# Attention block on one core: compressed and selected probabilities in 24 to 80 columns a head, transposed two or four heads at a time, against values laid out at the matching rows

## What is computed

```python
ck, cv = weighted sums of 16-token blocks of k, v (plus a position term)   # 64 blocks
a_comp = masked_softmax(q @ ck.T, block finished before the token)         # up to 64 columns
a_sel  = masked_softmax(q @ k_sel.T, token not before the key)             # 16 columns
a_win  = masked_softmax(q @ k.T, the last 128 tokens)
out = g0 * (a_comp @ cv) + g1 * (a_sel @ v_sel) + g2 * (a_win @ v)
```

## Time and profile before

| what | value |
|---|---|
| three runs shown | 2268.36, 2272.89, 2275.06 us, median 2272.89 |
| span of the profiled execution | 2265.8 us; no time is given for this execution by itself |
| PE, PEld | 2108.9 us (93%), 1398.6 us (62%) |
| DVE, ACT, POOL | 1698.7 us (75%), 1331.8 us (59%), 792.1 us (35%) |
| cs transposes (L645) | 1024 matmuls, in 256 groups of four |
| cs copies (L1127) | 256, of which 224 from the spare bank: 133.0 us |
| the three stretches | prologue to about 156 us, seven batches of 268.7 us, epilogue from about 2036 us |

### The profile page before, as it was taken

The page is one execution under the profiler, slowest core; times in us unless marked ns, Lnnn a source line. Parts: engine busy times, 40 slices in busy tenths (PEclk is TensorE's granted clock), DMA queues, the critical chain, the costliest instruction groups (busy, mean ns, idle before and its releaser), DMA issues.

```text
span 2265.8 us, 49116 instructions
## 1 busy us (share of the span) xinstructions
PE 2108.9 (93%) x17948; PEld 1398.6 (62%) x17948; DVE 1698.7 (75%) x4741; ACT 1331.8 (59%) x4706; POOL 792.1 (35%) x780
## 2 busy tenths in 40 slices
PE   6989999999999999999999999999999999997887
PEld 3656666566665666656665666656666566664454
DVE  4667777777876887777887777777787688776775
ACT  2346666656664665656665665655666566565554
POOL 2433333433334333333343333343333333333121
PEclk9999999999999999999999999999999999998999
DMA  6110000200011000110002000020001100021000
GB/s 219 55 34 25 20 29 29 70 30 29 24 49 55 25 20 30 52 47 29 29 24 75 29 19 26 29 70 29 29 25 52 52 25 20 29 52 38 20 21 19
DMA packets 49022, 89.66 MB, mean 40 GB/s; under 512 B 6888, under 2 KB 6888, under 8 KB 48784
## 3 DMA queue, kind: packets, MB, share of 16 engines
q1 hardware_dynamic: 37520, 68.95, 9.9%
q10 hardware_dynamic: 11264, 17.57, 2.1%
HBM read 69.68 MB, written 16.83 MB: 38 GB/s over the span
## 4 chain that ended last, share of the span: by engine, by line
PE 57%; DVE 26%; ACT 7%; issue 6%; POOL 3%; DMA 1%; SPq 0%; DVEq 0%; POOLq 0%; ACTq 0%
PE ps_m L719 9%; PE ps_o L651 7%; PE ps_m L684 5%; ACT pw L1093 5%; DVE ps_s L1632 4%; PE ps_s L645 4%; PE ps_m L523 4%; PE ps_m L525 4%; PE ps_m L524 4%; PE ps_t L627 4%; DVE wmax L1637 3%; PE ps_m L701 3%; PE ps_s L603 2%; DVE cden L1692 2%; DVE pT L1660 2%
## 5 line engine op out<-in xcount | busy, mean ns | idle before, releaser
L1093 ACT ACTIVATE pw<-ps_s,wmax 128x128 f32<-128x128 f32 x1024 | 359.1, 379 | 241.1 <-DVE wmax L1637 240.1
L523 PE MATMUL ps_m<-w_hi,h_hi 128*128 128x512 f32 x768 | 368.1, 479 | 4.0 <-DVE h_lo L1763 1.4
L1103 ACT ACTIVATE pw<-pw,wden 128x128 f32<-128x128 f32 x1024 | 313.8, 401 | 6.5 <-DVE wden L1647 6.1
L525 PE MATMUL ps_m<-w_hi,h_lo 128*128 128x512 f32 x768 | 303.6, 395 | 0.0
L524 PE MATMUL ps_m<-w_lo,h_hi 128*128 128x512 f32 x768 | 303.6, 395 | 0.0
L684 PE MATMUL ps_m<-wo_s,aT 128*128 128x512 f32 x512 | 259.3, 628 | 6.4 <-ACT v_s L1058 3.7
L719 PE MATMUL ps_m<-wbt_s,h2T 128*128 128x512 f32 x512 | 252.2, 612 | 0.0
L1127 ACT ACTIVATE pT<-ps_s 80x512 f32<-80x512 f32 (+6 forms) x224 | 133.0, 594 | 182.2 <-PE ps_s L645 171.5
L1093 ACT ACTIVATION_READ_ACCUMULATOR pw<-ps_s,wmax 128x1 f32 x1024 | 224.6, 219 | 0.0
L1658 DVE COPY_PREDICATED pT<-keep_prev,ps_t 128x512 f32<-128x512 uint32 x224 | 163.8, 731 | 52.9 <-PE ps_t L627 51.5
L1345 POOL TENSOR_TENSOR css<-css,cm 128x256 f32<-128x256 f32 (+7 forms) x128 | 110.9, 887 | 258.6 <-DVE cm L1684 258.6
(11 more groups left out here) (196 smaller groups left out, 4219.5 us busy)
## 6 DMA issues: line engine op xcount, KB each, us to landing
xa<-x_in SPq DMA_DIRECT2D x65, 256.0 KB, 2.9
xc<-x_in SPq DMA_DIRECT2D x64, 256.0 KB, 2.7
out<-t ACTq DMA_DIRECT2D x64, 256.0 KB, 2.1
wo_s<-wo_in SPq DMA_DIRECT2D x8, 1024.0 KB, 9.3
wbt_s<-wbt_in SPq DMA_DIRECT2D x8, 1024.0 KB
gbc<-gate_rows SPq DMA_DIRECT2D x24, 256.0 KB, 5.2
pw<-wmod_in SPq DMA_DIRECT2D x3, 1024.0 KB, 8.0
pT<-wmod_in SPq DMA_DIRECT2D x3, 1024.0 KB, 9.2
```

The costliest lines, as they stand in the source:

```text
L523: pe_.matmul(ps[:], h_hi[:, c, :], w_hi[:, col, c, :], start=(c == 0), stop=False)
L525: mm = pe_.matmul(ps[:], h_lo[:, c, :], w_hi[:, col, c, :], start=False, stop=(c == NC - 1))
L1093: ins = act.activation(pw[:, hw, :], ps_w[:, j, i, 1, :], ACT.Exp, bias=wmax[:, hw:hw + 1], accum_out=wden[:, 0, hw:hw + 1])
L1103: act.activation(pw[:, hw, :], pw[:, hw, :], ACT.Copy, scale=wden[:, 2, hw:hw + 1]).then_inc(wn_ok, 1)
```

## The change

- `css` holds the heads at a width that depends on the tile (`head_width`): 32 columns for tiles 0 and 1, 64 for tiles 2 to 5, 80 for tiles 6 and 7, the heads in the order of their group. `csp` is gone; exponentials and scaling happen in place, `cs_exps` and `cs_mask` are one instruction each.
- A transpose takes 128 columns, four heads at a width of 32 and two at 64, and one head's 72 or 80 columns in tiles 6 and 7. So a tile needs 1, 2 or 4 rounds of four transposes and a copy (`rounds_of`), 18 a batch where there were 32. `transpose_cs` and `probs_copy` return at once for rounds that a tile doesn't have; the calls stay where they were.
- A head's probabilities then lie at rows 32j or 64(j mod 2), so its values must lie there too: `cs_values` reads `cv_four` (tiles 0 and 1), `cv_two` (tiles 2 to 5) or `csv` (6 and 7). SP makes these copies of `csv` by six DMAs a batch, 512 KB (`spread_values`, L447 and L449 of the new kernel), put at the head of a batch's loop; `cs_values` of tile 0 waits for them (`d_cv`).
- `compress` writes the values at rows 16 to 79 in three strips of 32 instead of two, `select_values` adds to the first strip, and one ACT copy replaces two.

```diff
+def head_width(t):
+    return 32 if t < 2 else 64 if t < 6 else CS
+def rounds_of(t):
+    return 1 if t < 2 else 2 if t < 6 else 4
...
+            def spread_values(b):
+                sp.wait_ge(cv_done, b + 2)
+                for k in range(2):
+                    sp.dma_start(cv_two[64 * k:64 * k + 64, :], csv[0:64, :]).then_inc(d_cv, 16)
+                for k in range(4):
+                    sp.dma_start(cv_four[32 * k:32 * k + 32, :], csv[0:32, :]).then_inc(d_cv, 16)
             def batch(b, a):
                 for s in range(1, NT):
+                    if s == 1:
+                        spread_values(b)
...
-            def transpose_cs(b, t, g):
+            def transpose_cs(b, t, r):
+                if r >= rounds_of(t):
+                    return
...
-                rows = P - NB + blocks_seen(t)
-                for j in range(4):
-                    mm = pe_.transpose(dst[0:rows, j, :], csp[:, NC * j + g, 0:rows], ident)
+                wide, rows = (P, P) if w < CS else (CS, NSEL + blocks_seen(t))
+                for k in range(4):
+                    at = wide * (4 * r + k)
+                    mm = pe_.transpose(dst[0:rows, k, :], css[:, at:at + rows], ident)
...
-            def cs_values(b, t, g):
-                add_values(g, csv, pT_cs[:, g % 2], False, True, P - NB + blocks_seen(t)).then_inc(pvc_done, 1)
+            def cs_values(b, t, c):
+                if t == 0 and c == 0:
+                    pe_.wait_ge(d_cv, 16 * REPLICAS * (b + 1))
...
+                    src, at, part = ((cv_four, 32 * j, c) if rounds == 1 else
+                                     (cv_two, 64 * (j % 2), 2 * (c % 2) + j // 2) if rounds == 2 else (csv, 0, j))
+                    mm = pe_.matmul(ps_o[HD * j:HD * j + HD, c, :], src[at:at + n, cols], pT_cs[at:at + n, k % 2, part, :],
+                                    start=False, stop=True, skip_group_check=True)
...
-                act.activation(csp[:, :, 0:NSEL], css[:, :, 0:NSEL], ACT.Exp).then_inc(cs_exp, 1)
-                n = blocks_seen(t)
-                act.activation(csp[:, :, P - NB:P - NB + n], css[:, :, NSEL:NSEL + n], ACT.Exp).then_inc(cs_exp, 1)
+                v = heads(t)[:, :, 0:NSEL + blocks_seen(t)]
+                act.activation(v, v, ACT.Exp).then_inc(cs_exp, 1)
...
-                for p in range(2):
-                    ins = dve.tensor_tensor(css[:, 8 * p:8 * p + 8, 0:n].rearrange("p (j c) n -> p j c n", j=2),
-                                            ps_s[:, 2 * p:2 * p + 2, 0:4 * CS].rearrange("p j (c n) -> p j c n", c=4)[:, :, :, 0:n],
-                                            mask, ALU.add)
+                dve.tensor_tensor(css[:, 0:H * head_width(t)].rearrange("p (c j n) -> p c j n", c=NC, j=4)[:, :, :, 0:n],
+                                  ps_s[:, :, 0:4 * CS].rearrange("p j (c n) -> p j c n", c=NC)[:, :, :, 0:n],
+                                  csmask[:, t, 0:n].unsqueeze(1).unsqueeze(1).broadcast_to([P, 4, NC, n]), ALU.add
+                                  ).then_inc(s_done, 1)
```

More of the change, by code:

```diff
@@ L151, in blocks_seen, with rounds_before, values_through, value_strip @@
     return (t + 1) * (P // CB)
-def t_spare(t, g):
-    return t > 0
+def head_width(t):
+    return 32 if t < 2 else 64 if t < 6 else CS
+def rounds_of(t):
+    return 1 if t < 2 else 2 if t < 6 else 4
+def rounds_before(T):
+    per = [rounds_of(t) for t in range(NT)]
+    return T // NT * sum(per) + sum(per[:T % NT])
+def values_through(k):
+    b, r = divmod(k, rounds_before(NT))
+    t = max(u for u in range(NT) if rounds_before(u) <= r)
+    return 4 * (NT * b + t) + (r - rounds_before(t) + 1) * 4 // rounds_of(t)
+def value_strip(t):
+    return divmod(NSEL + t * (P // CB), 32)
 def program(nc, x, wqkv, wo, wbt, wa, wb, cT, wmod, bo, bg, rb, wcomp, pe, pet, wg, const, gscr, out):
@@ L224, in program @@
         csv = sb("csv", [P, D])
+        cv_two = sb("cv_two", [P, D])
+        cv_four = sb("cv_four", [P, D])
         csk = sb("csk", [P, NC, CS])
@@ L554, in compress @@
                     pe_.wait_ge(s_done, QUADS * ba + quad(0, 1) + 2)
-                    for k in range(2):
-                        pe_.matmul(strip[k], pew[:, 0:per], pe_s[:, :], start=True, stop=False, skip_group_check=True)
+                    for k in range(3):
+                        at = NSEL if k else 0
+                        pe_.matmul(ps_cv[32 * k:32 * k + 32, :], pew[:, at:at + 32], pe_s[:, :], start=True, stop=False,
+                                   skip_group_check=True)
                 for t in tiles:
-                    if t == half - 1:
+                    if t == NT - 1:
                         pe_.wait_ge(*m_done_at(seg, b, "V", NT - 1))
[L560 to L565, removed]
+                    k, row = value_strip(t)
+                    off = NB - 8 - row
+                    pe_.matmul(ps_cv[32 * k:32 * k + 32, :], blkw[:, off:off + 32], v_s[:, t, :], start=False,
+                               stop=(t in (5, 7)), skip_group_check=True)
             def importance(ba):
@@ L1119, in copy_zT, with probs_copy @@
                 act.activation(zT[:, :], ps[0:NZ + 1, 0:P], ACT.Copy).then_inc(done, 1)
-            def probs_copy(b, t, g):
-                n = 4 * (NT * b + t) + g
-                act.wait_ge(tc_full, n + 2)
-                if g >= 2 or t > 0:
-                    act.wait_ge(pvc_done, n)
-                rows = P - NB + blocks_seen(t)
-                act.activation(pT_cs[0:rows, g % 2], (spare_t if t_spare(t, g) else ps_t)[0:rows], ACT.Copy).then_inc(tc_done, 1)
+            def probs_copy(b, t, r):
+                if r >= rounds_of(t):
+                    return
+                k = rounds_before(NT * b + t) + r
+                act.wait_ge(tc_full, k + 2)
+                if k >= 2:
+                    act.wait_ge(pvc_done, values_through(k - 2) + 1)
+                rows = P if head_width(t) < CS else NSEL + blocks_seen(t)
+                act.activation(pT_cs[0:rows, k % 2], (spare_t if t else ps_t)[0:rows], ACT.Copy).then_inc(tc_done, 1)
             def copy_out(b, t):
@@ L1689, in cs_factor @@
                 base = CS_STEPS * T
-                dve.wait_ge(cs_exp, 2 * T + 3)
-                for w, (lo, n) in enumerate(((0, NSEL), (P - NB, blocks_seen(t)))):
-                    dve.tensor_reduce(cden[:, w, :], csp[:, :, lo:lo + n], AX.X, ALU.add).then_inc(cs_ok, 1)
+                dve.wait_ge(cs_exp, T + 2)
+                for w, (lo, hi) in enumerate(parts(t)):
+                    dve.tensor_reduce(cden[:, w, :], heads(t)[:, :, lo:hi], AX.X, ALU.add).then_inc(cs_ok, 1)
                 dve.wait_ge(cs_ok, base + 6)
```

96 lines of the change are left out of this document (48 added, 48 removed).

## The result

The changed kernel takes 2319.95 us (median of 4 runs, 2318.94 to 2324.0) against 2272.1 us of the kernel before (4 runs): 1.0214 times the time, 95% interval 1.0199 to 1.0228. That is 48 us slower, where 11.7 us faster was forecast.

The account below looks back on a forecast made before the run. The prediction took PE as the bound, with waits for DVE. Its terms, -6.2 - 2.0 + 3.2 - 2.7 - 4.0 = -11.7 us, took 2272.9 to 2261 us, range 2249 to 2279.

Parts of the forecast that it names:

- What bounds the kernel: PE first, busy 93% of the span; work taken from it counts only where PE is late, as it sometimes awaits DVE.
- signs that were to show me wrong: Slots 2 to 5 losing over 0.6 us or gaining time, PE waiting over 3 us, or cv_four values far over 0.22.
- First slot, tile 0: cs_values 0 waits for the six copies, delaying the next scores by 0.53 us in six batches: +3.2 us.
- the rival of late copies: The six copies reach first-slot cs_values 0 late; 4.2 us instead of 0.7 would give 2282 us; chance 0.24.
- Slots 2 to 5: 28 loop slots: 0.55 us won at the window's last transposes, 0.33 lost to changes of shape behind: -6.2 us.
- The prices: On PE, a group of four cs transposes takes 0.44 us and each change of matmul shape costs 0.11.
- ACT's copies at nothing: 14 fewer ACT copies a batch, 112 x 0.6 us, counted as no gain in the loop because ACT has time there.
- the turn at nothing: At the turn, three compression strips side by side instead of two, and six more SP issues, were to cost nothing.
- Tile 1: In the first slot, the second norm's transposes come 0.38 us sooner, later savings and shape changes cancelling: -2.7 us.
- The mask: One DVE instruction for two saves 0.07 us at the head of slots 2, 5, 6 and 7: -2.0 us.
- The epilogue: Last batch's slots: -1.4 us in the first slot, smaller gains in tile 1 and later slots: -4.0 us in all.
- Strips on different rows: Rival: cs_values strips on different rows don't run side by side, 70 us more, giving 2321 us; chance 0.08.

Follow-up runs that it names:

- run 1: Changed kernel with SP issuing the six copies of the compressed values ahead of the feed-forward weights instead of behind: 2287.73 us, ratio 1.0055.
- run 3: Changed kernel with the packing undone: all tiles in four rounds of 80 columns, values at one set of rows, no copies: 2293.89 us, ratio 1.0083.
- run 5: Kernel of run 3 with cs_values of tiles 2 to 5 reading 72 rows instead of 40 to 64: 2280.63 us, ratio 1.0016.
- run 2: Changed kernel with POOL's product of the keys held behind DVE's second norm in first slot and turn: 2309.88 us, ratio 1.0155.
- run 4: Kernel before with ACT's copy of the keys ahead of the second copy of compressed probabilities in the first slot: 2279.22 us, ratio 1.0017.
- run 9: Changed kernel with edits of run 1 and run 2, cs_values 0 and 1 before the window's last transposes, DVE's t before the gates' second half: 2262.78 us.

## Why the prediction was wrong, by its steps

- **What bounds the kernel**: right as a rule, not carried through. I had written that work taken from PE counts only where PE is late, and then looked at one bank. Two of the signs that were to show me wrong came: slots 2 to 5 got longer, and in the first slot PE waited over 3 us (3.99).
- **First slot, tile 0** (+3.2, measured +27.7) is the step with most of the error. The mechanism was named, as the rival of late copies, and weighed too lightly. I had sized the copies by bytes at 373 GB/s, and let only 0.26 MB of their 0.52 count; behind the weights they cost 2.5 us, 212 GB/s. I had also read the end of the old transfers from the bytes, 972.2, where `xa` landed at 972.95. The issues were mis-sized too, 4.5 us for six where I had 2.4, but they were over 3.9 us before the last copy landed and did not set it. `cs_values` started 1.9 us later than forecast, 3.3 later than before, and I had no term for the clock, which took 1 us more after the stop of 4 us (run 1: both go together).
- **Slots 2 to 5** (-6.2, measured +8.6). The prices were right: changes of shape at 0.11 us, three of them behind the wait, and with the 0.02 behind each they account for run 3 and run 5. The gain of 0.55 was the wrong step. It was real at the first bank (27.55 to 27.01), but 0.43 us behind it stands a second one that DVE gives back only at 27.9, so 0.08 was left. DVE's timeline had that row; I asked for the wait of the next instruction and not of the one behind.
- **ACT's copies at nothing, the turn at nothing** (measured +0.9 us in tile 1 and +0.85 in the turn, 12 us): here I asked what ACT's absence would cost and not what it would set off. ACT's earlier copy let POOL start into DVE's norm (runs 2 and 4). The Trainium skill says this plainly (SBUF — State Buffer, SBUF: two separate sides): the second pair of ports of DVE, which GpSimd shares, is an exclusive lock for a whole instruction, where the DVE instruction uses two ports or reads two operands from SBUF. The trace agrees: 1.48 us for 0.55, ending behind POOL's 1.27; that the norm is such an instruction, no run shows by itself. It was a rule against this change that I did not weigh. Its clause that the one that starts first gets the lock holds only roughly by the starts in the profile, which are rough for POOL: DVE lost it with a lead of 0.05 to 0.10 us. Why POOL came some hundredths earlier in the turn stays open.
- **Tile 1** (-2.7): at full clock and without the collision it took 23.97 us (run 2) for 24.04, so 0.07 of the 0.38 was there. The norm's transposes came 0.28 us earlier (11.52 us after the slot's start for 11.80), but the changes of shape behind them were not paid for by the third group, as I had it: 0.21 went again.
- **The mask**: the price was right, 1.49 us for the pair's 1.55 in tile 7. Slot 6 is 0.11 us shorter; slot 7 with the turn, without the collision (run 2), is not (62.87 for 62.82), so how much of the 2.0 us was paid stays open.
- **The epilogue** (-4.0, measured +1.1): its first slot also waits for the copies. In run 1 it takes 20.64 us for 21.87, close to the -1.4 forecast; the slots behind it vary by more than a microsecond with the clock in all kernels, so the rest can't be told.
- **Strips on different rows** run side by side: that rival fell. By the Trainium skill (TensorEngine Tiling, Gotcha 1: PSUM Pressure) different row tiles cannot use one bank at the same time; here two or four of them wrote one bank, at other partitions, 7 ns one after the other as in the kernel before, with no such price.

## What to carry to other kernels

Where work is taken from the bounding engine, follow it to the next two or three banks that another engine has to give back; the gain ends at the first that is late, and it came here only with the edit that made that engine earlier (run 9). A small copy is priced by what stands ahead of it in its queue, not by its bytes alone, and the stop of 4 us that it made on PE cost 1 us of clock on top. An engine that gets faster off the path starts something earlier: look at what runs on the other engines at that moment, above all POOL against DVE.

## What the runs showed of the hardware

- A DMA from SBUF to SBUF of 32 or 64 rows took mostly 0.50 to 0.60 us of SP's time to issue, at most 1.9, with next to nothing queued ahead (run 1), and 0.5 to 1.4 behind the weights; the weights' 1 MB took 0.38. One of 32 rows landed 2.0 us after its issue began with next to nothing ahead, 5.3 behind the weights (medians).
- Matmuls of 24 to 64 rows are a shape of their own: between them and those of 128 rows the pitch, from one's start to the next one's, was 200 ns, between 72 to 112 rows and 128 it was 89 (runs 3 and 5, and the kernel before). Behind such a change the second round over the four strips comes after 113 ns, later ones after 89.
- DVE's norm and POOL's product shut each other out, which cost a norm of 0.55 us another 0.93 to 1.09, and a lead of 0.10 to 0.13 us decided for DVE.
